# The hand-over from the Mamba stage to the expert stage: the plan of the early tiles, their loads and tile 0's first work are put into the last scan and into the last sequence's tail

## The chip, the cores and the metric

One core of a Trainium2 chip. The metric is device time in microseconds (us). Engines: PE is TensorE, DVE VectorE, ACT ScalarE, POOL GpSimd, SP SyncE, which here only issues DMAs.

## The reference

Eight sequences of 512 tokens with 256 channels. Cut to its order:

```
x = layernorm(x + mamba(x))      # mamba ends in a layernorm of its own:
    # project in, 4-tap convolution, silu; B, C and dt from it
    # h[t] = h[t-1] * exp(dt*A) + dt*B*x;  y = sum over 16 states of h*C + x*D
    # y * silu(gate), project out, + x, layernorm
x = layernorm(x + ffn(x))        # 8 experts, top 4 of them for each token:
    # out = down(min(gate,7) * sigmoid(1.702*gate) * (clip(up,-7,7)+1)), weighted, summed
```

## The kernel before

It has three stages. **Stage 1** (to about 590 us) works by rounds, `ROUNDS`, from -1 to 9 (`r.like`), each of 16 slots `t`. In round r sequence r is scanned (`r.b`), r+1 is projected in (`r.a`), r-1 is projected out and normed twice (`r.c`), and r-2 is routed to its experts (`r.d`). Rounds 8 (`SEQS`) and 9 (`LAST`) scan nothing: they are the tail of the last two sequences. Each engine has a hand-written order over rounds and slots; semaphores tie the engines together. In a slot DVE weighs the inputs of one of the 16 states (`weigh_inputs`) and scans it (`scan`), POOL multiplies the state by C (`read_state`), and PE sums (`sum_states`). The weights of experts and the rows of tile 0 share memory with what stage 1 uses: `first_raw`, `first_wh` and `first_wl` hold the input and two of the four broadcast rings (`bc`).

Routing of a sequence: transposes of its normed rows (`transpose_rows`), router product (`route`), ranking on DVE (`rank_experts`), a count over tokens on PE (`count`, `take_counts`), places in the experts' queues (`places`), and sixteen indirect DMAs by POOL that scatter its rows to the queues in device memory (`scatter`). `while_scanning` makes POOL wait at some slots so that it doesn't run beside certain DVE work.

**Stage 2** takes the queues in tiles of 512 rows of one expert (36 tiles in these runs, in pairs; the first `EARLY` = 4 are written out, the rest is a loop). For each tile SP loads its expert's weights and rows (`load_weights`, `load_rows`). Products are made in split precision: ACT copies a value to fp32r (`copy_weights`, `copy_tile`, `copy_product`) and DVE subtracts for the remainder (`rest_of_...`), and PE multiplies high by high, high by low and low by high. A tile has four chunks of up-projection (`up_projection`, read by `read_gate`, `read_up`; `clip_up`, `product_of_chunk` on DVE) and four of down-projection. DVE reads the output (`read_output`), ACT weighs it, POOL adds it to `total` with four indirect adds (`add_output`). DVE's copy of a tile's token numbers, `copy_tokens`, waits for the adds of the tile two before.

Which expert and which rows tiles 0 to 3 take is worked out on DVE by `plan_early`, from the counts of the first `EARLY_SEQS` = 6 sequences, by some 16 small steps that each wait for the one before; `plan_rest` plans the others in stage 2. The early tiles hold only full tiles. The constants for it (`c_tile`) are loaded over a buffer of stage 1. At the end of each order:

```
for _ in range(12): next(plan)        # DVE, round 8, slot 0: 12 steps of plan_early
weave(plan)                           # DVE, round 8, slot 2, behind the gate
if r.d and t == (4 if r.last else 3): count(r)       # PE, ahead of project_out at slot 3
LAST_SCATTERS = {6: (0,), 7: (1,), 10: (2,), 12: (3,), 13: range(4, TT * TOPK)}   # POOL
```

`weave` runs several chains of steps in turn. **Stage 3** (from about 1302 us) is the last layernorm, sequence by sequence.

## Time and profile before

| | us |
|---|---|
| median of 3 runs | 1333.25 (1333.24 to 1339.11) |
| the profiled execution | 1337.31 |
| its span, first to last instruction | 1335.5 |
| busy: PE, DVE, ACT, POOL | 1170.2, 1048.7, 896.6, 745.3 |

Busy times are sums over the span. The end of the last scan is at 572.4 us of the span, the first down-projection at 631.0 and the first add to `total` at 661.6. Times in the text without another unit are us from the start of that span.

### The profile page before, as it was taken

The page shows a single profiled execution, that of the slowest core. Times are in us where ns is not written, and L with a number is a line of the kernel's source. Part 1 is how long each engine was busy: PE and PEld are TensorE (multiplying, and loading weights), DVE is VectorE, ACT ScalarE, POOL GpSimd, SP SyncE. Part 2 cuts the span into 40 slices and gives each one's busy share as a digit, 9 for nine tenths or more (in the row PEclk, how much of TensorE's full clock was granted, in tenths as well). Part 3 has the DMA queues.
Part 4 walks back from the last instruction along what each step waited for, and adds up shares of the span by engine and source line. Part 5 has one row for each costly group of instructions (what it writes and reads, how often), then busy time and mean ns, then how long its engine had stood idle before and what let it go on. Part 6 is the DMA issues. An engine that isn't in the chain of part 4 may idle for free. (4 is left out here: it accounts for less than half of the span.)

```text
span 1335.5 us, 17897 instructions
## 1 busy us (share of the span) xinstructions
PE 1170.2 (88%) x5138; PEld 805.3 (60%) x5138; DVE 1048.7 (79%) x1791; ACT 896.6 (67%) x1551; POOL 745.3 (56%) x566
## 2 busy tenths in 40 slices
PE   7879897979898897676899999999999999999940
PEld 3324353534353434245788888888888888888830
DVE  2999999999999999964777667777677777766734
ACT  3785959495959585516577766777676777766734
POOL 0356567888787878967633444443444433444442
PEclk9899998999999898977899999999999999999975
DMA  2543444445454545354866556556556566556637
GB/s 74 217 179 127 154 148 177 176 166 187 173 191 172 192 154 181 127 192 157 315 164 161 133 139 165 160 162 162 128 140 167 160 162 163 138 135 161 162 36 252
DMA packets 69260, 217.21 MB, mean 163 GB/s; under 512 B 7520, under 2 KB 43232, under 8 KB 56288
## 3 DMA queue, kind: packets, MB, share of 16 engines
q1 hardware_dynamic: 29664, 167.42, 34.4%
q0 software_dynamic: 26880, 36.72, 16.1%
q10 hardware_dynamic: 12672, 12.58, 2.9%
q8 instruction: 16, 0.26, 0.1%
q14 instruction: 28, 0.23, 0.0%
HBM read 165.54 MB, written 51.15 MB: 162 GB/s over the span
## 5 line engine op out<-in xcount | busy, mean ns | idle before, releaser
L640 PE MATMUL p_y<-read,small 128*128 128x512 f32 x512 | 257.8, 642 | 58.2 <-POOL read L1187 58.2
L1051 DVE TENSOR_TENSOR_SCAN state<-decay,p_bu 128x512 f32<-128x512 f32 x256 | 297.3, 1203 | 1.5 <-issue 1.5
L1511 POOL DMA_INDIRECT total<-o_v,tok x144 | 267.4, 1857 | 44.1 <-issue 44.0
L640 PEld LDWEIGHTS p_y<-read,small 128*128 128x128 f32 x512 | 101.3, 205 | 199.5 <-issue 116.8
L1509 POOL TENSOR_TENSOR scrap<-neg_half 128x1 f32<-128x1 f32 x36 | 13.6, 379 | 319.9 <-ACT o_v L1418 317.3
L824 ACT ACTIVATE decay<-dt,scan_rate 128x511 f32<-128x511 f32 x256 | 164.3, 710 | 10.1 <-DVE state L1051 9.8
L504 ACT ACTIVATE gate_v<-p_g,bias 128x512 f32<-128x512 f32 x144 | 98.4, 683 | 102.8 <-PE p_up L494 97.7
L1229 POOL DMA_INDIRECT queues<-rows,index x128 | 133.4, 1042 | 32.5 <-issue 29.2
L1405 ACT ACTIVATE ah<-a_v 128x512 fp32r<-128x512 f32 x144 | 91.1, 633 | 89.6 <-DVE a_v L518 85.9
L1187 POOL TENSOR_TENSOR read<-state,bc 128x1024 f32<-128x1024 f32 x64 | 127.5, 2004 | 20.7 <-DVE p_bu L1042 8.4
L512 DVE TENSOR_SCALAR up_v<-up_v 128x512 f32<-128x512 f32 x144 | 61.4, 427 | 68.5 <-ACT up_v L507 65.9
L1456 DVE TENSOR_TENSOR al<-a_v,ah 128x512 fp32r<-128x512 f32 x144 | 98.8, 686 | 12.4 <-ACT ah L1405 12.4
L518 DVE SCALAR_TENSOR_TENSOR a_v<-gate_v,up_v 128x512 f32<-128x512 f32 x144 | 99.7, 693 | 4.9
L507 ACT ACTIVATE up_v<-p_up,bias 128x512 f32<-128x512 f32 x144 | 98.2, 682 | 0.0
L1187 POOL TENSOR_TENSOR read<-state,first_wh 128x1024 f32<-128x1024 f32 x32 | 64.0, 2001 | 59.6 <-DVE p_bu L1042 53.8
L1187 POOL TENSOR_TENSOR read<-state,first_wl 128x1024 f32<-128x1024 f32 x32 | 63.9, 1997 | 39.9 <-DVE p_bu L1042 15.6
L1378 PE MATMUL p_o<-first_wh,ah 128*128 128x256 f32 x288 | 82.6, 287 | 2.3 <-DVE al L1456 2.3
L1378 PE MATMUL p_o<-wh,ah 128*128 128x256 f32 x288 | 81.9, 284 | 1.7 <-DVE al L1456 1.7
L1042 DVE TENSOR_TENSOR p_bu<-p_u,bc 128x512 f32<-128x512 f32 x128 | 81.3, 681 | 0.0
L1378 PE MATMUL p_o<-first_wl,ah 128*128 128x256 f32 x288 | 80.8, 281 | 0.0
L1378 PE MATMUL p_o<-first_wh,al 128*128 128x256 f32 x288 | 80.8, 281 | 0.0
L1378 PE MATMUL p_o<-wh,al 128*128 128x256 f32 x288 | 80.3, 279 | 0.0
(220 smaller groups left out, 3017.6 us busy)
## 6 DMA issues: line engine op xcount, KB each, us to landing
bc<-bc_rows SPq DMA_DIRECT2D x32, 1024.0 KB, 4.7
first_raw<-in_w_experts SPq DMA_DIRECT2D x19, 1668.0 KB
raw_w<-in_w_experts SPq DMA_DIRECT2D x18, 1668.0 KB
first_wh<-bc_rows SPq DMA_DIRECT2D x16, 1024.0 KB
first_wl<-bc_rows SPq DMA_DIRECT2D x16, 1024.0 KB
first_rows<-queues SPq DMA_DIRECT2D x19, 544.0 KB
xq<-queues SPq DMA_DIRECT2D x18, 544.0 KB
queues<-pad SPq DMA_DIRECT2D x9, 544.0 KB
```

Source lines behind the costliest of these rows:

```text
L504: act.activation(gate_v[i % 2][:, :], p_g[i % 2][:, :], ACT.Silu, bias=bias[t.p][:, 0, i:i + 1], scale=ALPHA)
L507: act.activation(up_v[i % 2][:, :], p_up[i % 2][:, :], ACT.Identity, bias=bias[t.p][:, 1, i:i + 1])\
L518: dve.scalar_tensor_tensor(a_v[i % 2][:, :], gate_v[i % 2][:, :], TOP, up_v[i % 2][:, :], ALU.min, ALU.mult)\
L640: mm = pe.matmul(p_y[h][:, :], ident[:, :], read[:, t % 4, h, :], start=False, stop=(t == SLOTS - 1))
L824: act.activation(decay[t % AHEAD][:, h, 1:LEN], dt[s.p][:, h, 1:LEN], ACT.Exp, scale=rate[:, h, t:t + 1])\
L1051: dve.tensor_tensor_scan(state[t % 4][:, h, :], decay[t % AHEAD][:, h, :], p_bu[:, h * LEN:(h + 1) * LEN], 0.0, ALU.mult, ALU.add).then_in ...
L1187: pool.tensor_tensor(read[:, t % 4, :, :], state[t % 4][:, :, :], of_state(t, 1), ALU.mult).then_inc(s_read, 1)
L1229: pool.indirect_dma_start(queues, bass.IndirectOffsetOnAxis(ap=index[s.p][:, i:i + 1], axis=0), rows[s.p][:, i // TOPK, :], None).then_inc ...
L1378: mm = pe.matmul(to, v[:, i, a * P:(a + 1) * P], w[t.p][:, c:c + D], start=(i == 0 and a % 2 == 0 and m == 0), stop=(i == CH - 1 and m == ...
L1405: act.activation(ah[:, i, :], a_v[i % 2][:, :], ACT.Copy).then_inc(s_ah, 1)
L1456: dve.tensor_tensor(al[:, i, :], a_v[i % 2][:, :], ah[:, i, :].bitcast(F32), ALU.subtract).then_inc(s_al, 1)
L1511: pool.indirect_dma_start(total, bass.IndirectOffsetOnAxis(ap=tok[t.p][:, a:a + 1], axis=0), o_v[t.p][:, a, :], None, compute_op=ALU.add). ...
```

## The change

- **Plan**: five sequences, not six, fill the early tiles. `plan_early` is woven with `rank_experts` in round 7 (the last scan), slot 2; POOL waits there for its end (`s_tables`). `c_tile` is loaded in that scan, ahead of its fifth broadcast.
- **Tile 0's loads** are issued when SP has done the last scan's broadcasts; writing the spare rows goes behind the loads of tiles 0 and 1.
- **Tile 0's work**: ACT copies its weights at the start of round 8, DVE's remainders, the tile's transposes and its split follow in slots 0 to 3; all four chunks of up-projection (`AHEAD_OF_LOOP = CH`) are issued on PE in slot 4 of round 8, behind `count`, which is behind `project_out` now. The first two are read at slot 6, the others in round 9, where three products are split too. Two of three parts of tile 1's weights are also done before stage 2.
- **POOL**: two scatters of sequence 5 go from the last slot of round 7 to behind the reads in round 8.

The helpers `copy_product` and `rest_of_product` are moved out of stage 2's functions unchanged.

```diff
         d, a, c = self.d, self.a, self.c
-        return (["tr0", "tr1", "rt"] * d + ["in0", "in1"] * a + ["cnt"] * d + ["o0", "o1"] * c + ["cv0", "cv1"] * a
-                + ["dt0", "dt1", "bc", "in2", "in3"] * a)
+        scanning, over = d and self.b, d and not self.b
+        return (["tr0", "tr1", "rt"] * d + ["in0", "in1"] * a + ["cnt"] * scanning + ["o0", "o1"] * c + ["cnt"] * over
+                + ["cv0", "cv1", "dt0", "dt1", "bc", "in2", "in3"] * a)
...
-EARLY, EARLY_SEQS = 4, 6
+EARLY, EARLY_SEQS = 4, 5
 assert EARLY_SEQS * LEN * TOPK - E * (TILE - 1) > (EARLY - 1) * TILE
...
-        dve.wait_ge(s_tload, 16)
+        dve.wait_ge(s_dt, SEQS)
         dve.memset(one_row[:, :], 1.0)
...
         yield from steps.step(dve.tensor_tensor(early_first[:, :], early_upto[:, :], full_e[:, :], ALU.subtract))
+        dve.wait_ge(s_tload, 16)
         yield from list_tiles(dve, steps, 0, EARLY, early_upto, early_first, early_first)
...
-    AHEAD_OF_LOOP = 2
+    AHEAD_OF_LOOP = CH
...
                     sum_states(r.s.at(-1), SLOTS - 2 + t)
-                if r.last and t == 0:
-                    transpose_tile(pe, Seq(0, 0))
-                    up_projection(pe, Seq(0, 0), 0)
                 if r.d and t == 0:
...
                     route(r)
+                if r.like == SEQS and t == 2:
+                    pe.wait_ge(s_bu, halves_done(r.s, -1))
+                    transpose_tile(pe, Seq(0, 0))
                 if r.a and t == 2:
...
                     project(r, 1)
-                if r.last and t == 4:
-                    up_projection(pe, Seq(0, 0), 1)
-                if r.d and t == (4 if r.last else 3):
+                if r.d and r.b and t == 3:
                     count(r)
...
                     project_out(r, 1)
+                if r.d and not r.b and t == 4:
+                    count(r)
+                if r.like == SEQS and t == 4:
+                    for i in range(AHEAD_OF_LOOP):
+                        up_projection(pe, Seq(0, 0), i)
                 if r.a and t == 4:
...
+                if r.like == SEQS and t == 3:
+                    act.wait_ge(s_y, SEQS)
+                    for k in range(KD):
+                        copy_tile(act, first, k)
+                if r.last and t == 3:
+                    copy_product(act, first, 0)
+                    copy_product(act, first, 1)
+                    for i in (2, 3):
+                        read_gate(act, first, i)
+                        read_up(act, first, i)
+                    copy_product(act, first, 2)
                 if r.d and t == 3:
...
-                if r.like == SEQS and t == 8:
-                    act.wait_ge(s_y, SEQS)
+                if r.like == SEQS and t == 0:
+                    act.wait_ge(s_read, SLOTS * (SEQS - 1) + 4 * RING - 4)
                     for i in range(3):
-                        copy_weights(act, Seq(0, 0), i)
-                    for k in range(KD):
-                        copy_tile(act, Seq(0, 0), k)
+                        copy_weights(act, first, i)
+                if r.last and t == 0:
+                    copy_weights(act, second, 1)
                 if r.d and t == 0:
...
                     store_x1t(r, 1)
-                if r.last and t in (1, 4):
-                    read_gate(act, Seq(0, 0), t // 4)
-                    read_up(act, Seq(0, 0), t // 4)
                 if r.a and t == 2:
...
                     apply_norm(r.s.at(-1), 0, z, s_normed1)
+                if r.like == SEQS and t == 6:
+                    for i in (0, 1):
+                        read_gate(act, first, i)
+                        read_up(act, first, i)
+                    copy_weights(act, second, 0)
                 if r.like == Round.FIRST and t == 7:
...
         plan = plan_early(dve, plan_steps)
+        early, second = Seq(0, 0), Seq(0, 1)
         for r in ROUNDS:
             for t in range(SLOTS):
-                if r.like == SEQS and t == 0:
-                    for _ in range(12):
-                        next(plan)
                 if r.like == Round.FIRST and t == 2:
...
                     gate(r)
-                if r.like == SEQS and t == 2:
-                    weave(plan)
-                if r.last and t == 1:
-                    clip_up(dve, Seq(0, 0), 0)
-                    product_of_chunk(dve, Seq(0, 0), 0)
                 if r.d and t == 2:
                     route_steps = Steps(dve, s_route, r.s.at(-2).n, ROUTE_STEPS)
-                    weave(rank_experts(r, route_steps))
-                if r.d and t == (5 if r.last else 3):
+                    weave(rank_experts(r, route_steps), *[plan] * (r.like == SEQS - 1))
+                if r.like == SEQS and t == 0:
+                    for i in range(2):
+                        rest_of_weights(dve, early, i)
+                if r.like == SEQS and t == 2:
+                    rest_of_weights(dve, early, 2)
+                if r.like == SEQS and t == 3:
+                    for k in range(KD):
+                        rest_of_tile(dve, early, k)
+                    read_bias(dve, early)
+                if r.like == SEQS and t == 10:
+                    for i in (0, 1):
+                        clip_up(dve, early, i)
+                        product_of_chunk(dve, early, i)
+                    rest_of_weights(dve, second, 0)
+                if r.last and t == 3:
+                    rest_of_weights(dve, second, 1)
+                    rest_of_product(dve, early, 0)
+                    rest_of_product(dve, early, 1)
+                    for i in (2, 3):
+                        clip_up(dve, early, i)
+                        product_of_chunk(dve, early, i)
+                    rest_of_product(dve, early, 2)
+                if r.d and t == (3 if r.b else 5):
                     take_counts(r, route_steps)
...
                     make_padding(dve)
-                if r.last and t == 0:
-                    for i in range(2):
-                        rest_of_weights(dve, Seq(0, 0), i)
-                    for k in range(KD):
-                        rest_of_tile(dve, Seq(0, 0), k)
-                    read_bias(dve, Seq(0, 0))
                 if r.last and t == 5:
...
                 pool.wait_ge(s_rexp, 2 * r.s.at(-2).n + 1)
+            if r.like == SEQS - 1 and t == 2:
+                pool.wait_ge(s_tables, 1)
             if r.d and t == 6:
...
             for t in range(SLOTS):
-                if r.d and r.b and t in SCATTERS:
+                if r.d and r.b and t in SCATTERS and not (r.like == SEQS - 1 and t == SLOTS - 1):
                     scatter(r.s.at(-2), SCATTERS[t])
...
                 if r.like == SEQS and t == 0:
-                    scatter(r.s.at(-3), range(9, TT * TOPK))
+                    scatter(r.s.at(-3), range(SCATTERS[SLOTS - 1][0], TT * TOPK))
                 if r.c and t == 6:
...
             for pair in range(PAIRS):
+                if i == SEQS - 1 and pair == RING:
+                    sp.wait_ge(s_u, SEQS)
+                    sp.dma_start(c_tile.rearrange("p a b -> p (a b)"), ins["tile"]).then_inc(s_tload, 16)
                 if r.b:
...
             for i in range(CH):
-                if i > 0:
-                    copy_product(t, i - 1)
-                elif later:
-                    copy_product(t.at(-1), CH - 1)
+                if later:
+                    copy_product(act, t.at(-1) if i == 0 else t, (i - 1) % CH)
                 if later or i >= AHEAD_OF_LOOP:
...
                     copy_share(t, expert)
-                if i == 0:
+                if i == 0 and later:
                     copy_weights(act, t.at(1), 0)
...
                         copy_tile(act, t.at(1), k)
-                    copy_weights(act, t.at(1), 1)
+                    if later:
+                        copy_weights(act, t.at(1), 1)
                 if i == 2 and later:
...
         end = Seq(ends[0], 1)
-        copy_product(end, CH - 1)
+        copy_product(act, end, CH - 1)
         weigh_output(end)
...
         plan = plan_rest(dve, plan_steps)
-
-        def rest_of_product(t, i):
-            n = CH * t.n + i
-            dve.wait_ge(s_ah, n + 1)
-            dve.tensor_tensor(al[:, i, :], a_v[i % 2][:, :], ah[:, i, :].bitcast(F32), ALU.subtract).then_inc(s_al, 1)
...
             for i in range(CH):
-                if later or i > 0:
+                if later:
                     clip_up(dve, t, i)
...
                     copy_tokens(t)
-                    rest_of_weights(dve, t, 2)
+                    if later:
+                        rest_of_weights(dve, t, 2)
                 if i == 1 and later:
...
                         rest_of_tile(dve, t.at(1), k)
-                if i == 2:
+                if i == 2 and later:
                     rest_of_weights(dve, t.at(1), 0)
...
                     read_bias(dve, t.at(1))
-                rest_of_product(t, i)
+                if later or i == CH - 1:
+                    rest_of_product(dve, t, i)
         assert next(plan, "end") == "end"
...
             for i in range(2):
-                sp.wait_ge(s_scat[i], 16 * TT * TOPK * (seqs // 2))
-
-        sp.wait_ge(s_u, SEQS)
-        sp.dma_start(c_tile.rearrange("p a b -> p (a b)"), ins["tile"]).then_inc(s_tload, 16)
+                sp.wait_ge(s_scat[i], 16 * TT * TOPK * ((seqs + 1 - i) // 2))
+
         sp.wait_ge(s_silu, 2 * SEQS)
...
         load_weights(sp, Seq(0, 0))
-        sp.wait_ge(s_ends, 2)
-        write_spare_rows(sp)
         scattered(EARLY_SEQS)
...
         load(Seq(0, 1))
+        sp.wait_ge(s_ends, 2)
+        write_spare_rows(sp)
         for t in tiles(sp, ends):
```

## Rows read from the trace of the kernel before

**Rows 1.** Waits, 710 to 1290: engine, line <- releaser: us, times, longest.

```profile
POOL scrap L1509 <- ACT o_v L1418: 291.6, 32, 9.2
...
DVE tok L1461 <- DMA total<-o_v,tok: 93.2, 31, 3.7
```

**Rows 2.** Timeline of DVE: start, us, work [idle before <- releaser].

```profile
707.70 0.17 DVE L1461 CAST tok<-first_rows 128x4 uint32<-128x4 int32 x1 [2.78 <-DMA total<-o_v,tok]
```

**Rows 3.** Instructions of line L1461: ns min/median/max, first to last start.

```profile
L1461 DVE CAST tok<-xq x18: 165/170/172, 649.3 to 1271.6; 128x4 uint32<-128x4 int32 x18
```

**Rows 4.** Timeline of POOL, last sequence's scatters and first add.

```profile
628.97 0.99 POOL L1229 DMA_INDIRECT queues<-rows,index  x1 [0.16 <-issue]
...
651.72 0.96 POOL L1229 DMA_INDIRECT queues<-rows,index  x1 [0.30 <-issue]
...
660.33 1.08 POOL L1509 TENSOR_TENSOR scrap<-neg_half 128x1 f32<-128x1 f32 x1 [7.65 <-ACT o_v L1418]
```

**Rows 5.** Timeline of DVE around the last scan's end.

```profile
570.11 2.31 DVE L1051 TENSOR_TENSOR_SCAN state<-decay,p_bu 128x512 f32<-128x512 f32 x2
...
572.96 6.64 DVE L426 CAST rest<-used_i 128x8 f32<-128x8 int32 x1
...
581.75 1.29 DVE L1059 TENSOR_TENSOR y<-p_y,sg 128x512 f32<-128x512 f32 x2
...
583.54 0.23 DVE L416 CAST row_i<-rest 128x4 int32<-128x4 f32 x1
```

**Rows 6.** Timeline of POOL around the last scan's end.

```profile
567.22 3.96 POOL L1187 TENSOR_TENSOR read<-state,bc 128x1024 f32<-128x1024 f32 x2
...
573.65 3.96 POOL L1187 TENSOR_TENSOR read<-state,bc 128x1024 f32<-128x1024 f32 x2
```

**Rows 7.** Timeline of PE between the stages.

```profile
569.28 8.41 PE L640 MATMUL p_y<-read,small 128*128 128x512 f32 x12 [2.29 <-POOL read L1187]
...
577.53 1.04 PE L664 MATMUL p_bank<-small,rows 128*128 128x128 f32 x8
...
580.12 1.85 PE L674 MATMUL p_bank<-small,x1t 128*128 128x8 f32 x16
...
586.11 2.05 PE L597 MATMUL p_bank<-w,y 128*128 128x256 f32 x4
...
594.05 1.03 PE L597 MATMUL p_bank<-w,y 128*128 128x256 f32 x4
...
595.22 0.70 PE L656 MATMUL p_bank<-x,small 128*128 128x256 f32 x2
...
640.54 0.76 PE L494 MATMUL p_g<-xh,wh 128*128 128x512 f32 x1 [4.21 <-issue]
```

**Rows 8.** Groups of DVE instructions, 672 to 1300: xcount | busy, mean ns.

```profile
L1456 DVE TENSOR_TENSOR al<-a_v,ah 128x512 fp32r<-128x512 f32 x136 | 93.3, 686 | 12.0 <-ACT ah L1405 12.0
...
L468 DVE TENSOR_TENSOR wl<-raw_w,wh 128x1024 fp32r<-128x1024 f32 x51 | 60.9, 1222 | 0.2
```

**Rows 9.** Windows: us, busy by engine, then PEclk, DMA share, GB/s.

```profile
590.00:592.00 2.00, 2.00 (x6) 1.04 (x5) 0.00 (x0) 0.00 (x0) 0.00 (x0) 0.50 0.99 379
```

**Rows 10.** Timeline of ACT and POOL at the last sequence's second norm.

```profile
606.87 1.11 POOL L1197 TENSOR_TENSOR neg_16th<-row_sum,norm_c 128x4 f32<-128x4 f32 x1 [0.26 <-DVE z L1067]
...
613.00 2.08 ACT L861 ACTIVATE rows<-z,neg_mean,rstd 128x256 f32<-128x256 f32 x4 [1.78 <-POOL neg_mean L1206]
```

**Rows 11.** Timeline of DVE around the last ranking.

```profile
620.11 0.57 DVE L512 TENSOR_SCALAR up_v<-up_v 128x512 f32<-128x512 f32 x1 [9.51 <-ACT up_v L507]
...
621.32 0.18 DVE L1075 TENSOR_TENSOR lg<-p_bank,small 128x32 f32<-128x32 f32 x1
...
627.91 0.18 DVE L1160 CAST index<-spot_sum 128x16 uint32<-128x16 f32 x1
```

**Rows 12.** Timeline of SP's queue in the last scan.

```profile
507.56 7.54 SPq L1321 DMA_DIRECT2D bc<-bc_rows  x2
```

**Rows 13.** DMA issues, 480 to 680: KB each, us to landing.

```profile
expo<-in_tile SPq DMA_DIRECT2D x1, 168.0 KB, 5.1
```

More of the change, by code:

```diff
@@ L519, in product_of_chunk, with copy_product @@
            .then_inc(s_a, 1)
+    def copy_product(act, t, i):
+        n = CH * t.n + i
+        act.wait_ge(s_a, n + 1)
+        after(act, s_down, n - CH + 1)
+        act.activation(ah[:, i, :], a_v[i % 2][:, :], ACT.Copy).then_inc(s_ah, 1)
     def copy_tile(act, t, k):
@@ L530, in rest_of_tile, with rest_of_product @@
            .then_inc(s_xl, 1)
+    def rest_of_product(dve, t, i):
+        n = CH * t.n + i
+        dve.wait_ge(s_ah, n + 1)
+        dve.tensor_tensor(al[:, i, :], a_v[i % 2][:, :], ah[:, i, :].bitcast(F32), ALU.subtract).then_inc(s_al, 1)
     def read_bias(dve, t):
@@ L734, in act_stage1 @@
     def act_stage1(act):
+        first, second = Seq(0, 0), Seq(0, 1)
         def load_table(func):
@@ L1399, in act_stage2 @@
         ends = []
-        def copy_product(t, i):
-            n = CH * t.n + i
-            act.wait_ge(s_a, n + 1)
-            after(act, s_down, n - CH + 1)
-            act.activation(ah[:, i, :], a_v[i % 2][:, :], ACT.Copy).then_inc(s_ah, 1)
         def copy_share(t, expert):
@@ L1451, in dve_stage2 @@
         plan = plan_rest(dve, plan_steps)
-        def rest_of_product(t, i):
-            n = CH * t.n + i
-            dve.wait_ge(s_ah, n + 1)
-            dve.tensor_tensor(al[:, i, :], a_v[i % 2][:, :], ah[:, i, :].bitcast(F32), ALU.subtract).then_inc(s_al, 1)
         def copy_tokens(t):
```

## Prediction

> **What bounds the kernel now.** I read the waits of the second stage first. Over nearly all of it POOL waits for the scaled output of a tile, and DVE waits for earlier adds to land before it copies the next tile's token numbers [rows 1]. The timeline of one tile shows that this is a closed loop: DVE's copy at 707.7 is released by the landing of an add [rows 2]; behind it in DVE's order stands the reading of the tile before, which ACT scales and POOL adds, and the landing of that releases the next such copy. The copies of tiles 1 and 35 are 622.3 us apart, 18.3 us a tile [rows 3]. No other engine closes that period: so the second stage ends at the time of its first add plus a fixed number of periods, and the change, which touches none of the loop's members, is worth what it does to the **first add**. The reader is to look at what releases that add: before, POOL has sat idle for 7.65 us, waiting for tile 0's output, when it starts at 660.33; its sixteen scatters of the last sequence ran from 628.97 to 652.7 [rows 4]. So two chains arrive there: the scatters, and tile 0.
>
> **The change, part by part.**
>
> *The plan moves into the scan.* Before, it starts as the last scan ends (572.4) and its last step is at 583.5 with the gate's two products in between; of that span 6.64 is one cast [rows 5]. That cast lies under POOL's two last reads and the operation behind them [rows 6]. Without the stall (6.5) and the gate (1.2) the plan is 11.2 + 0.2 - 6.5 - 1.2 = 3.7, plus the hand-overs around it. In the scan DVE is never idle, so all of it moves the scan's end, less a few tenths for being woven into the ranking. I take **3.8 later** (bounds: 3.0 if the weaving hides the ranking's share, 4.8 with a scatter's length, about 1 us, of stall). POOL is held until the plan is done, so no read can lock the casts out; it resumes with DVE, as it did, and I charge nothing more.
>
> *Behind the scan.* The reads of the last two states stood behind two scatters, from 571.2, when the reads before end, to 573.65 [rows 6]. These scatters now follow the reads. But PE is the later one: its sums of three states run from 569.28 to 577.7 at a slow clock, so the last sum, which ends as the router product starts at 580.1, comes only some 0.1 sooner than the shift [rows 7]: 583.8. DVE's subtraction of the early weights (two halves, 1.22 each [rows 8]) meets these reads. The long cast shows what happens: DVE waited until 579.6, through all that POOL had lined up [rows 5, 6]. Here DVE would wait to 580.9 and be done at 583.3, before the last sum. I charge nothing; if that cover fails, up to 2.4. The Trainium skill (SBUF — State Buffer, Who interferes with whom) says that a DVE instruction with two SBUF inputs and a GpSimd one that reads SBUF exclude each other for one whole instruction, whoever starts first. By that rule DVE could get in between two reads and put the last read off by 1.2 to 2.4, which speaks against the change; the last sum would then still start within 0.3 of the same time, since PE has the sum before it and the transposes to do.
>
> The gate ends at 585.1, 2.1 later than before. Then the gain: before, PE stood idle from 582.0 to 586.1, for the ranking and the count, and projected from 586.1 to 595.9, more than half of it at a clock of 0.5 [rows 7, 9]. Now the count stands behind the projection, and the router product (1.85) and tile 0's transposes (1.1, eight of them, like the eight of 577.53) fill PE until 586.7. PE has then been busy without a gap since the sums, so I take the full clock that it had reached by 580: the last quarter of before, 594.05 to 595.9, is 1.7 and a tail of 0.15, four are 6.9, and end at **593.6, 2.3 earlier**. At the slow clock it is 9.8, ending at 596.5, 0.6 later.
>
> *Norms of the last sequence.* From there to the end of the second norm took 19.2 (595.9 to 615.1 [rows 7, 10]). Added: the index of sequence 6 now waits for the late count, and POOL's first scatter of it stands ahead of the reciprocal root, 0.6. Removed: the mean's two small products took 1.1 each, as the first shows [rows 10], under DVE's subtraction of the weights; now a shorter clip is there, -1.2. So 612.2, 2.9 earlier. The first two chunks lie in this stretch in which PE was idle. The other two wait for ACT to read the first pair after the first norm; they restart after an idle of 4 us, one of them slow, and end at about 612, just as the transposes of the last sequence are due.
>
> *The last ranking.* Before, 6.2 passed from the norm to the ranking's first operation at 621.32, since ACT and DVE had the first chunk in front of it [rows 10, 11]. The clip and product just ahead of it (1.2, from 620.11) are gone from there, and I take 0.6 off for the end of the first chunk on PE, which the transposes had to wait for: 4.4, 616.6. From there to the index took 6.8 [rows 11]. Now DVE has, between ranking and counts, one half of the weights (1.2), three product remainders (0.6 each with overlap [rows 8]) and two clips with products (1.1 each, 620.11 to 621.32 with a slower start [rows 11]), 5.2 where it waited 2.6 for the count: 9.4. The index comes at **626.0, 2.1 earlier**. POOL's scatters of sequence 6 have to be gone by then; they start behind the second power, 2.9 earlier, and before they ended exactly when the last sequence's began. Before, 24.1 passed from POOL's small operation ahead of the first of them (628.6) to the last one's end [rows 4]; 626.0 + 0.2 + 24.1 gives POOL free at **650.3**.
>
> *Tile 0 and 1.* Tile 0 now has three of four products split before the stage begins, and the early weights of tiles 0 and 1 are done; only tile 1's x remainder stands between the index and tile 1's first chunk: 626.0 + eight plan steps at 0.23 (3.7 over 16 steps) 1.8 + the token copy 0.1 + two remainders 1.3 = 629.2, against 640.54 [rows 7]. Tile 0's output follows from it at the old distance, 19.8 to POOL's start at 660.33 [rows 4]: 649.0. That is before 650.3, by 1.3. All loads of SP (weights 0, rows 0, weights 1) are asked sooner than before and are behind nothing new except the small table.
>
> **The sum.** The first add goes from 660.33 to 650.3: 7.65 of idle gone and the scatters 2.4 earlier, together 10.0. The profiled execution took 1337.31 with a span of 1335.5; the median shown is 1333.25, 4 below it and within its runs' spread. The gain is taken off the median: **1323.2**.
>
> **Rivals.**
> 1. *Tile 0 binds*, or the scatters go faster: the last sequence's sixteen took 1.48 each, 23.7 from the first start to the last end [rows 4]; if the new ones are 10% quicker, POOL is free at 647.9 and tile 0's 649.0, or 647 if PE's chunks run fast, sets the start: gain 11.3 to 13.3, 1320 to 1322. For: one scatter alone is 0.96 long, so they do wait for something. Against: these writes move with them. Chance 0.13.
> 2. *PE's clock stays at 0.5 in the projection*, or 2 to 3 us are lost in one of the new orders (DVE's 5.2 ahead of the counts is the nearest): the index comes at 628 to 629 and the gain is POOL's idle alone, 7: 1326. For: the clock was 0.5 behind an idle of 4 us [rows 7, 9]. The Trainium skill (TensorE: Matmul & The Clock Gate, HAM oscillation — how this bites in real kernels) says the same, that PE, after a gap, works its next burst slowed; by it the four chunks in two bursts pay twice. Against: no such gap is left ahead of the projection. Chance 0.20.
> 3. *The DMAs.* Eight padding writes, weights and rows of tiles 2 and 3 now fall on more of the scatters. At 1.7 to 1.85 a scatter instead of 1.48, POOL is free at 654 to 656: gain 4 to 6, 1328. Chance 0.12.
> 4. *No effect*: the loop isn't closed by the adds in the first tiles, and tile 1's chain, 1.3 ahead of the scatters here, is really held at its old place. Against: the wait of each following tile names the adds. Gain under 3: 1332. Chance 0.07.
> 5. *Slower.* The table of tile numbers lands late. It is asked behind the fourth broadcast, whose issue ends at 515.1, and takes 5.1 to land [rows 12, 13]: 520.3, and the plan wants it about 1.5 later. DVE waits there with the scan behind it, so each us goes straight to the end. It takes all of the gain only if it lands after 532, and shows as slower than 0.5% after 538: 1334 to 1345. Chance 0.06.
>
> **How the numbers follow.** My forecast (gain 8.5 to 11.4) has 0.42; its own range is 1321.5 to 1325. About 0.5% (6.7 us) is what a measurement of this kernel can tell from no change. Faster by more: my case, rival 1, and most of rival 2 (0.13), 0.68. Within: the rest of rival 2, rivals 3 and 4, 0.26. Slower: 0.06. The range 1319 to 1330 leaves out rivals 4 and 5 and the tails of 1 and 3, about 0.18.
>
> **What would show it.** In the new profile: no cast over 1 in the plan and the scan's last operation 3.8 later; the projection ended near 593.6 at a clock of 1.0; the last index near 626; POOL's idle ahead of its first add gone, or nearly so, with the last scatter just in front; that add near 650.3, and 18.2 a tile after it. The prediction is wrong if DVE idles in the last scan (rival 5), if POOL still waits for tile 0, or if the first token copy that waits isn't released by an add.

## Result, and the profile after

The changed kernel takes 1329.01 us, the median of 20 executions (1324.2 to 1337.13), against 1335.94 (1332.93 to 1341.28) for 20 of the kernel before, taken beside it: a ratio of 0.995, with a 95% interval of 0.9935 to 0.9964. That is 6.9 us faster where the forecast said 10.0. The time lies in the range of 1319 to 1330, which was set against a median of 1333.25; the kernel before read 2.7 more in the larger set. Taken as gains from 1333.25 that range is 3.3 to 14.3, so 6.9 lies in it as well. The gain of 10.0 doesn't lie in the measured interval, 4.8 to 8.7.

The profiled execution of the changed kernel took 1335.48, span 1333.6, and is one of the slowest of its 20. It is the profile of the change, so it comes first; one of an execution of the same kernel that took 1323.89 comes in the experiments. The steps at the end of the scan went as forecast. Timeline of DVE:

```profile
576.62 6.89 DVE L470 TENSOR_TENSOR first_wl<-first_raw,first_wh 128x1024 fp32r<-128x1024 f32 x2
584.36 1.29 DVE L1089 TENSOR_TENSOR y<-p_y,sg 128x512 f32<-128x512 f32 x2 [0.85 <-PE p_y L653]
...
619.08 0.19 DVE L1105 TENSOR_TENSOR lg<-p_bank,small 128x32 f32<-128x32 f32 x1 [10.00 <-PE p_bank L687]
...
628.37 0.17 DVE L1199 CAST index<-spot_sum 128x16 uint32<-128x16 f32 x1
```

No plan step stands there any more. In its place the two halves of the early weights take 6.89 where they need 2.35: the stall has moved from the plan's cast [rows 5] to this subtraction, as the prediction said, and it is hidden, since DVE, done at 583.5 (forecast 583.3), then waits 0.85 for PE all the same. POOL's order beside it:

```profile
571.48 7.85 POOL L1226 TENSOR_TENSOR read<-state,bc 128x1024 f32<-128x1024 f32 x4
579.30 1.99 POOL L1259 TENSOR_TENSOR x<-x,small 128x1024 f32<-128x1024 f32 x1
...
628.97 0.99 POOL L1268 DMA_INDIRECT queues<-rows,index  x1 [0.15 <-issue]
...
648.15 0.96 POOL L1268 DMA_INDIRECT queues<-rows,index  x1 [0.30 <-issue]
658.91 0.61 POOL L1543 TENSOR_TENSOR scrap<-neg_half 128x1 f32<-128x1 f32 x1 [9.81 <-ACT o_v L1456]
```

The last scatters take 20.1 (628.97 to 649.11), less than the 23.7 of [rows 4]. But POOL then idles 9.81 for tile 0's output, although tile 0 was meant to be early: the first add is at 658.91 and not at the 650.3 of the forecast. PE shows why:

```profile
586.77 1.03 PE L610 MATMUL p_bank<-w,y 128*128 128x256 f32 x4
...
593.05 0.70 PE L669 MATMUL p_bank<-x,small 128*128 128x256 f32 x2
...
642.49 0.28 PE L1422 MATMUL p_o<-first_wh,ah 128*128 128x256 f32 x1 [1.14 <-issue]
...
649.47 0.37 PE L1422 MATMUL p_o<-first_wl,ah 128*128 128x256 f32 x1 [1.03 <-issue]
```

The projection is right: four parts in 7.0, from 586.77 to 593.75, at a granted clock of 1.00 where [rows 9] had 0.50. The windows view of the stretch:

```profile
590.00:592.00 2.00, 2.00 (x10) 1.42 (x9) 0.68 (x4) 0.84 (x4) 1.42 (x2) 1.00 0.95 371
```

But from 640.06 to 651.60 PE gets through seven more recorded matmuls of tile 0's third down-projection, 1.0 to 2.1 us apart, and is idle in between for nothing that the profile can name ("issue"). In the same stretch SP spends 21.06 on issuing the eight padding writes:

```profile
630.95 21.06 SPq L577 DMA_DIRECT2D queues<-pad  x8
```

Whether this belongs to the change or to the execution is the first thing that the experiments ask. The second is why the gain is 6.9 and not 10.

### The profile page after: what moved, and what is told of

It reads as the page before. It is cut to its first block and busy times, and to the rows that moved or that the text cites. A ratio compares the mean times of both kernels' runs of the same rounds, so it can differ in the third digit from the quotient of the medians.

```text
span 1333.6 us, 17900 instructions
## 1 busy us (share of the span) xinstructions
PE 1165.7 (87%) x5138; PEld 803.6 (60%) x5138; DVE 1046.4 (78%) x1791; ACT 896.5 (67%) x1551; POOL 739.9 (55%) x566
## 5 line engine op out<-in xcount | busy, mean ns | idle before, releaser
L653 PEld LDWEIGHTS p_y<-read,small 128*128 128x128 f32 x512 | 100.6, 203 | 205.6 <-issue 112.2
L841 ACT ACTIVATE decay<-dt,scan_rate 128x511 f32<-128x511 f32 x256 | 164.3, 710 | 17.1 <-DVE state L1081 16.9
L527 ACT ACTIVATE ah<-a_v 128x512 fp32r<-128x512 f32 x144 | 91.0, 633 | 90.1 <-DVE a_v L520 83.6
L1226 POOL TENSOR_TENSOR read<-state,bc 128x1024 f32<-128x1024 f32 x64 | 127.3, 2000 | 22.4 <-DVE p_bu L1072 10.9
L514 DVE TENSOR_SCALAR up_v<-up_v 128x512 f32<-128x512 f32 x144 | 61.4, 426 | 65.4 <-ACT up_v L509 64.5
L1422 PE MATMUL p_o<-first_wh,ah 128*128 128x256 f32 x288 | 83.5, 290 | 6.3 <-DVE al L543 3.5
L1226 POOL TENSOR_TENSOR read<-state,first_wl 128x1024 f32<-128x1024 f32 x32 | 63.9, 1996 | 40.0 <-DVE p_bu L1072 17.1
```

The lines of the kernel that those rows point to most:

```text
L527: act.activation(ah[:, i, :], a_v[i % 2][:, :], ACT.Copy).then_inc(s_ah, 1)
L653: mm = pe.matmul(p_y[h][:, :], ident[:, :], read[:, t % 4, h, :], start=False, stop=(t == SLOTS - 1))
L841: act.activation(decay[t % AHEAD][:, h, 1:LEN], dt[s.p][:, h, 1:LEN], ACT.Exp, scale=rate[:, h, t:t + 1])\
L1226: pool.tensor_tensor(read[:, t % 4, :, :], state[t % 4][:, :, :], of_state(t, 1), ALU.mult).then_inc(s_read, 1)
L1422: mm = pe.matmul(to, v[:, i, a * P:(a + 1) * P], w[t.p][:, c:c + D], start=(i == 0 and a % 2 == 0 and m == 0), stop=(i == CH - 1 and m == ...
```

## Experiments

Times are read behind the end S of the last scan, since the first stage alone moves by up to 4 us from one execution to the next. The length of that scan, from its drive product (`p_u`) to S, stands in the second column. "Gate" is the end of the gate's products on DVE, "projected" the end of the projection out on PE, "last index" the end of the last sequence's index. All of the table is read from the timelines of DVE, POOL and PE of each profiled execution; "add 0" is the first add, "copy 2" and "copy 3" are the token copies of the third and fourth tile, which wait for landed adds.

| kernel | scan | gate | projected | last index | scatters end | add 0 | copy 2 | copy 3 |
|---|---|---|---|---|---|---|---|---|
| before | 65.8 | 10.6 | 23.5 | 55.7 | 80.3 | 87.9 | 99.4 | 117.4 |
| b_same | 65.9 | 10.6 | 22.4 | 52.0 | 84.1 | 84.1 | 94.6 | 112.7 |
| b_plan | 68.7 | 7.9 | 19.0 | 49.3 | 83.0 | 83.0 | 93.0 | 111.1 |
| b_count | 65.4 | 10.6 | 19.3 | 49.6 | 83.3 | 83.3 | 93.4 | 111.4 |
| b_plan_count | 68.7 | 7.9 | 15.1 | 45.9 | 71.7 | 75.6 | 86.7 | 104.7 |
| b_ends_late | 65.8 | 10.6 | 22.4 | 52.0 | 85.4 | 85.5 | 99.4 | 117.3 |
| after | 68.7 | 9.0 | 17.1 | 51.8 | 72.4 | 82.2 | 93.4 | 111.4 |
| a_same | 68.7 | 8.0 | 16.0 | 48.2 | 74.9 | 74.9 | 85.3 | 103.3 |
| a_count_old | 68.8 | 9.0 | 18.6 | 51.0 | 74.2 | 74.2 | 84.2 | 105.8 |
| a_ends_late | 68.7 | 8.1 | 15.8 | 48.7 | 72.9 | 73.0 | 86.8 | 104.8 |
| a_ends_twice | 68.8 | 8.0 | 15.9 | 48.8 | 73.2 | 83.5 | 93.7 | 116.0 |
| a_adds_early | 68.8 | 8.0 | 16.0 | 48.1 | 85.1 | 68.0 | 79.1 | 99.0 |
| a_both | 68.8 | 8.1 | 16.1 | 43.5 | 84.5 | 67.3 | 78.5 | 101.7 |
| a_weights_ahead | 68.7 | 8.0 | 16.0 | 48.1 | 83.6 | 67.2 | 78.9 | 100.6 |

**Is the starved PE part of the change?** The changed kernel was run again as it is, and with the padding writes moved or doubled, and the kernel before with them moved. Ratios are to the kernel before run beside each.

The kernel as it is, a_same:

> The changed kernel again, for the spread of one thing: in its first profile PE issued 16 instructions of tile 0's third down-projection chunk in 11.5 us (640.1 to 651.6, one about every 0.7 or 1.4), with nothing in the profile that it waited for, while SP issued the eight padding writes. Theory A (traffic): that gap is there in every execution, its length changes from run to run, and it is what spreads the times over 13 us. Theory B (an accident of one execution): it is mostly gone here. Under both the median is 5 to 8 us under the kernel before, and without the gap the first add stands at 648 to 650.

The eight padding writes one tile later, a_ends_late (and in the kernel before, b_ends_late); the two writes of spare rows get a semaphore of their own, so that the first add doesn't wait for the padding:

```diff
-            if isinstance(t.half, int) and t.n == 1:
+            if isinstance(t.half, int) and t.n == 2:
                 sp.wait_ge(s_ends, 3)
                 write_ends(sp, range(E))
```

> The changed kernel with its eight padding writes of the queues' ends issued behind the loads of tile 3 instead of those of tile 2, and the first add no longer waiting for them. Theory A (the padding writes starve PE of instructions): the gap of 11 us behind tile 1's first chunks goes, the first add stands at 648 to 650, and the time is 3 to 8 us under a_same, unless the same gap comes back beside the moved writes, then behind 655, where the adds' loop hides about 3 us of it. Rival (the gap belongs to that place in PE's program, or to the sixteen scatters): the gap stays at 640 and the time is a_same's within 1.5.

> The kernel before with the same late padding writes. Theory A: before had little of that gap (PE idle 4.2 at 640, which tile 1's weights explain), so 0 to 3 us faster than before at most. Then the change itself, measured between the two kernels with late padding, is worth about 10 us, as the forecast had it, and the missing 3 us are the gap. Rival: the two differ by 5 to 7 us as the unmodified pair does, and the missing gain is elsewhere.

The padding twice, a_ends_twice; the second eight go to a tensor that nobody reads:

```diff
                 write_ends(sp, range(E))
+                for e in range(E):
+                    sp.dma_start(sink[e * TILE:(e + 1) * TILE, :].rearrange("(p a) c -> p a c", a=SUBS), pad[:, :, :])\
+                      .then_inc(s_pad, 16)
```

> The changed kernel with eight more writes of 544 KB from the same padding tile to an unused part of device memory, right behind the eight. Theory A: the gap on PE grows by as much as the writes take longer, 8 to 12 us, and the first add, which waits for them too, comes at 668 or later: 6 to 12 us over a_same. Rival (the writes have nothing to do with it): the gap keeps its length; the first add is held only by the wait for the 16 writes, if they land after 659.

Measured: a_same 1323.72 against 1330.84 of the kernel before on the same chip, ratio 0.9942 (0.9923 to 0.9962), 7.1 faster. a_ends_late 1325.99 (0.9954, 0.9939 to 0.9969), a_ends_twice 1336.03 (1.0035, 1.0018 to 1.0053), b_ends_late 1337.59 (1.0044, 1.0027 to 1.006).

In the profiled execution of a_same PE isn't starved and SP needs 11.50 for the eight writes. Timeline of POOL, a_same:

```profile
621.54 0.99 POOL L1268 DMA_INDIRECT queues<-rows,index  x1
626.15 0.99 POOL L1268 DMA_INDIRECT queues<-rows,index  x1 [3.62 <-issue]
...
646.83 0.96 POOL L1268 DMA_INDIRECT queues<-rows,index  x1 [0.30 <-issue]
647.82 0.24 POOL L1543 TENSOR_TENSOR scrap<-neg_half 128x1 f32<-128x1 f32 x1
```

The first add follows the last scatter with no idle time. DVE starts to read tile 0's output at 63.0 behind S; from there to POOL's add 4.8 pass in b_plan_count, so tile 0 has some 7 us of slack, and the scatters set the first add. The starvation is in one of the eight profiles of the changed kernel and its variants. It is no fixed part of the change, and its cause stays open. The first theory for a_same, that it is in every execution, is out.

Nor is the padding a cost that moving it would save. Moved back, it falls on the adds: from the first add to the copy that waits for its landing 10.4 passed in a_same and 13.8 in a_ends_late. By the medians 2.3 is lost here, which the intervals don't tell from nothing, and 6.8 in the kernel before, which they do; b_ends_late was expected to be up to 3 faster. Between the two kernels with late padding the medians differ by 11.6, close to the 10 that the first theory expected there, but since the kernel before got slower and not since a loss went away. Doubled, the padding costs 12.3. Waits of a_ends_twice, 640 to 700 us:

```profile
DVE tok L1494 <- DMA total<-o_v,tok: 21.6, 2, 18.5
...
PE p_x L481 <- DMA xq<-queues: 17.0, 1, 17.0
```

PE waits 17.0 for the rows of a tile, queued behind the writes, where a_same waits 3.6. So the first theory, padding as the thing that ate the missing 3 us, isn't borne out: moving these writes back won nothing in either kernel. No run leaves them out, so what they cost where they are is not shown.

**Is the kernel before as its profile shows it?** b_same is the kernel before again, beside three variants of the changed kernel.

> The kernel before again, for a second profile of it, since the times of one kernel spread over 9 us. My sum took the first add from one execution, 87.9 us behind the end of its last scan (572.4), and b_ends_late, which is the same up to there, had it 85.5 behind. Theory (the sum started from a slow execution): the first add stands 84.5 to 86.5 behind the scan's end here, POOL's idle ahead of it is under 5, and the gain of the change, 143.6 from the last drive to the first add in a_same, is 7 to 8, not 10. Rival (the profiled execution was typical): 87 to 89, idle 7 or more.

Measured 1331.16 against 1330.64 (1.0001, 0.9986 to 1.0015). Its profiled execution was 7.3 quicker than the first profile of the same code, and differs from it in the very rows of [rows 4]. Timeline of POOL, b_same:

```profile
623.99 1.39 POOL L1229 DMA_INDIRECT queues<-rows,index  x1 [0.16 <-issue]
632.33 1.12 POOL L1229 DMA_INDIRECT queues<-rows,index  x1 [6.95 <-issue]
...
651.41 1.43 POOL L1229 DMA_INDIRECT queues<-rows,index  x1 [0.30 <-issue]
652.87 0.25 POOL L1509 TENSOR_TENSOR scrap<-neg_half 128x1 f32<-128x1 f32 x1
```

There is no idle time of POOL ahead of the first add, where [rows 4] have 7.65. Instead there is one of 6.95 between the first and the second scatter of the last sequence. The index is at 52.0 and not 55.7. POOL is 3.3 behind it with the last sequence's first scatter, since it is still at sequence 6's. The same picture, a pause of 6.75 to 6.95 and no wait for tile 0, is in the profiles of b_ends_late, b_plan and b_count. So four of the six profiles of the kernel before and its variants show it, and the one on which the prediction was built doesn't. The padding isn't the cause: in b_ends_late it is issued from 644.07 on, and the pause is there.

What goes with the pause is SP's load of the third tile's weights (1668 KB). Timeline of SP, b_same:

```profile
622.91 0.34 SPq L543 DMA_DIRECT2D first_raw<-in_w_experts  x1
624.05 0.34 SPq L552 DMA_DIRECT2D first_rows<-queues  x1
```

and of a_same, where that load is asked 28 us sooner, since the early weights are split sooner:

```profile
595.04 0.34 SPq L556 DMA_DIRECT2D first_raw<-in_w_experts  x1
622.26 0.34 SPq L565 DMA_DIRECT2D first_rows<-queues  x1
```

Where these weights are asked about 1.1 us ahead of the first scatter (b_same, b_ends_late, b_plan, b_count), the second scatter comes 8.1 to 8.3 after the first; where they are asked with it or behind it (the first profile before, b_plan_count), 2.6 to 2.9; where they were loaded long before (all kernels built on the changed one), 1.4 to 4.9. No kernel moved this load alone, so that it causes the pause is argued and not shown; nor is it shown why the pause varies from 0.44 to 3.9 among the kernels built on the changed one.

**Which part of the change does it?** First, the changed kernel with the count of sequence 6 back ahead of the projection out, a_count_old:

```diff
-                if r.d and r.b and t == 3:
+                if r.d and not r.last and t == 3:
                     count(r)
...
-                if r.d and not r.b and t == 4:
+                if r.last and t == 4:
                     count(r)
```

> The changed kernel with the count of sequence 6 back ahead of the projection (on PE, on DVE and in the order of the PSUM banks). The forecast gave this move 2.3 us together with the full clock. Theory: PE waits about 1.3 for the ranking ahead of the count and keeps its clock, so the projection ends about 1.5 later and the index 0.5 to 1 later: 0 to 1.5 us slower than a_same. Rival (without the move PE's clock falls as before and the projection ends 5 later): 3 to 4 us slower.

It took 1327.0 (0.9968, 0.9951 to 0.9984). That is 3.4 more than a_adds_early and 3.5 more than a_both, which ran beside it and stand for a_same (1323.72, another chip) as shown below; the intervals overlap, so a cost of the old place is likely and not certain. The projection ends at 18.6 behind S, where it ends at 16.0 in a_same and at 17.1 in the change's first profile, whose gate is as late as here: 1.5 to 2.6 are PE's wait for the ranking. Its four parts take 7.0 here too, so the clock is not what the count's place decides. The profiled execution took 1330.99, the slowest of its 12, and in it the later index doesn't reach the first add: the scatters behind it take 22.7 and not 26.3, and the add comes at 74.2, 0.7 sooner than in a_same. The delay is behind that add, where copy 3 comes 2.5 later than in a_same and PE waits longer for the rows of a tile than the 3.59 of a_same. Timeline of PE, a_count_old:

```profile
656.73 1.97 PE L480 MATMUL p_x<-small,xq 128*128 128x128 f32 x8 [5.28 <-DMA xq<-queues]
```

So this profile doesn't show that the count's place costs anything by way of the last index.

Then, from the other side, the kernel before with the plan's part alone (b_plan), with the count's place alone (b_count), and with both but nothing of tile 0's work moved (b_plan_count). In short:

```diff
-EARLY, EARLY_SEQS = 4, 6
+EARLY, EARLY_SEQS = 4, 5
...
-                    weave(rank_experts(r, route_steps))
+                    weave(rank_experts(r, route_steps), *[plan] * (r.like == SEQS - 1))
```

```diff
-                if r.d and t == (4 if r.last else 3):
+                if r.d and t == 3 and r.like < SEQS:
                     count(r)
                 if r.c and t == 3:
                     project_out(r, 0)
                     project_out(r, 1)
+                if r.d and t == 4 and r.like >= SEQS:
+                    count(r)
```

> The kernel before with the plan's part of the change alone: five sequences for the early tiles, the plan woven with the ranking in the last scan, its table loaded in that scan, POOL's wait, and two scatters moved behind the reads. The count, tile 0's work and SP's other orders stay as before. Theory: what counts is when the last index is ready. The last scan gets 2.9 us longer; the plan's 10 us behind the scan are gone, but only 2.6 of them lay on the path (gate at 8.0 behind the scan's end and not 10.6), because the projection stands behind the ranking and the count. So all comes 2.6 sooner behind a scan end that is 2.9 later: no change, 1331 within 1.5, and the index 49.4 behind the scan's end. Rival (the plan alone makes most of the gain, since the ranking too starts sooner and takes the projection with it): 1325 to 1327.

> The kernel before with one thing changed: in round 8 the count and the places of sequence 6 go behind the projection out. Theory: PE projects right behind the gate, at 18.6 behind the scan's end and not 22.4, and the last index, and with it the last scatters and the first add, come about 3 us sooner: 1328. Rival (the count only pays where PE has tile 0's transposes to keep busy with before it; here PE idles ahead of the gate, the clock is at half, and 8 us of projection eat the gain): 1330.5.

> Both parts together, and nothing of tile 0's work moved: tile 0's transposes, its split, its four chunks and tile 1's weights stand where they stood before. Theory (the last index and the sixteen scatters behind it set the first add; tile 0 has slack either way): index about 46 behind the scan's end, since the work that the change puts in front of the last counts is missing, first add 71 to 75 behind it, time 1321 to 1324.5, as fast as the whole change. Rival (tile 0 and tile 1 have to come sooner too): their chain binds, and the time is 1328 to 1331.

Measured, against 1330.62: b_plan 1332.76 (1.0007, 0.9989 to 1.0024); b_count 1327.78 (0.9992, 0.9976 to 1.0007); b_plan_count 1327.8 (0.9987, 0.9972 to 1.0002). None of the three can be told from no change by its ratio, though the medians of the last two are 2.8 lower. For the plan that was the expectation: all that follows comes 2.7 sooner behind a scan that is 2.8 longer. The count alone was expected to bring 3; its index comes 2.4 sooner, but POOL is still at sequence 6's scatters, the last sixteen take 30.2 where b_same has 28.9, and the first add comes 0.8 sooner. b_plan_count came out near the rival's 1328 and not at the theory's 1321 to 1324.5. Its scatters end at 71.7 as promised, but then tile 0 binds. Timeline of POOL, b_plan_count:

```profile
642.49 1.48 POOL L1228 DMA_INDIRECT queues<-rows,index  x1 [0.30 <-issue]
647.88 0.61 POOL L1513 TENSOR_TENSOR scrap<-neg_half 128x1 f32<-128x1 f32 x1 [3.91 <-ACT o_v L1422]
```

This is its fastest execution (1324.85), 1.0 above the profiled one of a_same; its median is 3 higher, and no profile shows what holds that. So in this execution tile 0's early work is what is missing, up to 3.9 at the first add. That it is only needed once the scatters end sooner fits b_same, where POOL doesn't wait for tile 0; the kernel before with tile 0's work alone was not run. None of the parts tried alone gives anything that its ratio tells from nothing, while the whole change does (a_same, 0.9942).

**Does the first add set the end?** POOL does ten of the last sixteen scatters, then tile 0's adds, then the other six, and the first add no longer waits for the padding (a_adds_early). In a_both DVE also takes the last counts ahead of the lot of products and weights that the change put in front of them.

```diff
             if r.last:
-                scatter(r.s.at(-2), range(TT * TOPK))
+                scatter(r.s.at(-2), range(FIRST_SCATTERS))
```

> The changed kernel with POOL's order changed in one place: ten of the last sequence's sixteen scatters, then tile 0's adds, then the other six; the first add waits for the spare rows alone and not for the padding of the queues. Theory (POOL's scatters set the first add, and the first add sets the end): tile 0's output is ready 66.5 behind the scan's end, so the first add comes there and not at 74.9, less 2 to 4 us that the adds take longer to land beside the padding: 4 to 8 us faster than a_same, about 1317 beside its 1323.7. Rival (something else holds the loop, the loads of tile 4 behind the last scatters above all): within 1.5 of a_same.

> As a_adds_early, and DVE works out the last sequence's counts, weights and index ahead of tile 0's product remainders and of chunks 2 and 3. Theory: the index comes 5 us sooner, but POOL is still at sequence 6's scatters then (they end 48 behind the scan), so the last scatters start at most 0.5 sooner; the early plan's successor, padding and token copy move 5 forward, tile 1's first chunk 2 to 4: the first add at 63 to 66 behind the scan, 0 to 3 us faster than a_adds_early. Rival (chunks 2 and 3 late cost as much as is won): 0 to 2 slower than it.

Measured: 1323.61 (0.9937, 0.9914 to 0.9961) and 1323.5 (0.9937, 0.9915 to 0.9959), both as a_same. The theory expected 1317, the rival the same as a_same. In a_adds_early the first add comes 7.0 sooner, copy 2 comes 6.2 sooner, but copy 3 only 4.3. Timeline of POOL, a_adds_early:

```profile
640.16 0.60 POOL L1546 TENSOR_TENSOR scrap<-neg_half 128x1 f32<-128x1 f32 x1 [3.38 <-ACT o_v L1459]
...
659.91 0.55 POOL L1546 TENSOR_TENSOR scrap<-neg_half 128x1 f32<-128x1 f32 x1 [2.67 <-ACT o_v L1459]
...
683.10 0.55 POOL L1546 TENSOR_TENSOR scrap<-neg_half 128x1 f32<-128x1 f32 x1 [14.49 <-ACT o_v L1459]
```

Three adds 19.8 and 23.2 apart; the third is at 683.10, as in a_same (110.9 behind S, 110.2 there). In a_both the index comes 4.6 sooner still, but the last sequence's first scatter is no sooner, at 48.8 behind S for 48.5. SP's waits in a_adds_early name what may have taken the gain back (590 to 690 us; in a_both the same wait is 19.2):

```profile
SPq L1588 <- DMA queues<-rows,index: 20.7, 1, 20.7
```

SP doesn't ask for anything of the fifth tile before the last scatter has landed, and the six scatters were put off. The last run asks for the fifth tile's weights ahead of that wait, a_weights_ahead:

```diff
                 sp.wait_ge(s_tables, 2)
+                load_weights(sp, t.at(1))
                 scattered(SEQS)
```

> The kernel with tile 0's adds ahead of the last six scatters, and the weights of tile 4 asked ahead of SP's wait for those scatters (its rows behind it). In the run before it the wait ended at 659.6, weights and rows were asked then, and PE waited 4.1 for the rows; the third tile's add came 23.2 behind the second's. Theory (these loads take back what the earlier adds give): the weights come some 8 us sooner, the rows land about 3 sooner, and 2 to 3 us of the 7 are kept: 1321 against 1323.6. Rival (the loop's buffers or the adds of tile 1, put off by six scatters, hold it): 1323.5, no change.

It took 1320.96 (5 executions, 1319.06 to 1324.05; 0.9944, 0.993 to 0.9957). The median is the lowest of all, but the ratio is that of a_same: no version here is shown to beat the changed kernel. The gap that was 23.2 is gone, and another has come ahead of it. Timeline of POOL, a_weights_ahead:

```profile
639.40 0.61 POOL L1546 TENSOR_TENSOR scrap<-neg_half 128x1 f32<-128x1 f32 x1 [2.65 <-ACT o_v L1459]
...
661.71 0.55 POOL L1546 TENSOR_TENSOR scrap<-neg_half 128x1 f32<-128x1 f32 x1 [5.86 <-ACT o_v L1459]
...
679.49 0.46 POOL L1546 TENSOR_TENSOR scrap<-neg_half 128x1 f32<-128x1 f32 x1 [9.07 <-ACT o_v L1459]
```

The third add is 3.6 sooner than in a_same here, 2.9 if counted from S. From there the tiles keep their pace. So the loads of the fifth tile were what made the 23.2, and part of the earlier first add is kept in this profile; whether it is in the median the ratio doesn't tell.

## Why the prediction was right, and where its size was off

**The frame held.** The second stage ends at its first add plus fixed periods. The waits of a_same, 710 to 1270 us, are those of [rows 1]:

```profile
POOL scrap L1543 <- ACT o_v L1456: 282.9, 31, 9.2
DVE tok L1493 <- DMA total<-o_v,tok: 93.7, 31, 3.7
```

From the fifth tile's token copy to the end of the span 626.2 to 629.5 pass in all fourteen profiles, while that copy itself stands between 691.0 and 709.6. The limit of the frame showed in a_adds_early: the loop carries an earlier first add only as far as the loads of the next tiles come too.

**The changed kernel was forecast well, by the profile of a_same.** From the start of the last scan the first add was to come after 143.7 (69.6 of scan and 74.1 behind it); a_same has 68.7 and 74.9, 143.6. Step by step, forecast and a_same: the plan lengthens the scan by 3.8, and by 2.8 to 2.9; the gate at 8.9 behind S, and 8.0; the projection ended at 17.4, and 16.0, at full clock; the last ranking at 40.4, and 38.7; the index at 49.8, and 48.2; the scatters done at 74.1, and 74.9, tile 0 ahead of them. The scatters took 26.3 where 23.7 were taken. In the change's own profile the prediction's sign of being wrong stood: POOL still waited for tile 0, 9.81, for the starved PE that no step of the prediction had. And the hit of 143.6 for 143.7 is partly luck: the scan came 0.9 shorter than forecast, the index 1.6 sooner behind it, and the scatters took 2.4 more.

**The term that was mis-sized is the starting point**: "7.65 of idle gone". POOL's idle time ahead of the first add stands in one of two profiles of the kernel before. In b_same the index came 3.7 sooner than in that profile and the first add 3.8 sooner, with the scatters up to it. Against b_same the sum is: scan +2.8, index 3.8 sooner, and from the index to the first add 26.7 for 32.1, 5.4 less; together 6.4, where 7.1 was measured and 10.0 forecast (+3.8, -5.9, -7.9). Most of the 3.6 between 10.0 and this sum of 6.4 is the 3.8 by which the first add stands later in the first profile than in b_same. The prediction took the term off the median, although it had noted that the profiled execution was 4 above it. That was against three executions; against the 20 of the larger set (1335.94) it is 1.4 above, and b_same is 1.1 under the median of its own set. So that the idle time is unusual is shown against the later sets (1330.6), where POOL waits for tile 0 in only one of the five profiles of the kernel before and its variants (b_plan_count's, 3.91); for the first set, which has no second profile of the kernel before and where 6.9 was measured all the same, it is argued.

So, between a_same and b_same, the gain has another make-up than told. It isn't idle time that goes. Of the 5.4 between index and first add, 2.8 are POOL's start, which stood behind sequence 6's scatters in b_same (3.3) and doesn't in a_same (0.4), and 2.6 are the sixteen scatters, 26.3 for 28.9; that comes from the shorter pause behind the first of them (3.6 for 6.95), whose cause is open. What each part of the change pays is shown less well: the count's place takes 1.5 to 2.6 off the projection, but a_count_old doesn't show it at the first add; the plan's place gains 2.7 and costs 2.8; without tile 0's early work POOL waits 3.9 in the fastest execution of b_plan_count.

**The rivals.** The first, tile 0 binding, is not so in a_same, and is so in the profile of the change, where PE is starved. The second, a slow clock in the projection, didn't happen in any profile of the changed kernel or its variants, not even in a_count_old. The third, slower scatters, happened in part: 1.64 each in a_same, with the pause, against 1.48 forecast, but 1.26 each in the changed kernel's first profile. For the fourth, no effect, nothing speaks: the ratio is clear of 1, and the token copies wait for landed adds. The fifth was out: DVE went through the plan without a pause. The lock between DVE and POOL was hidden, as its step said. The Trainium skill (SBUF — State Buffer, Who interferes with whom) lets either engine in after one whole instruction of the other. The trace doesn't agree with that: the record begins at 576.62, POOL's last operation ends at 581.29, and the two halves need 2.35 and end at 583.51, so DVE was held through the rest of the third read, the fourth and the operation behind them, more than one instruction. The prediction's own reading, DVE done at 583.3, was the right one.

## What to carry to other kernels

A profile is one execution: before a wait in it is booked as a gain, compare the profiled time with a median of more than three, and look at a second profile for the same wait, above all where two chains arrive within a few us of each other. Where two chains meet (here scatters and tile 0), moving one of them can leave the other to bind, as in b_plan_count, so the parts of such a change can't be priced one by one. An earlier start of a loop can be taken back by the loads of the following tiles, as the 7.0 of a_adds_early were by its third add.

## What the runs showed of the hardware

- PE fell to one recorded matmul per 1.0 to 2.1 us and SP to one DMA issue per 2.6 (1.3 to 1.5 in the other profiles), for 11 us or more, with nothing named that they wait for: in one profile of fourteen, at a DMA share of 0.32 to 1.02 over the stretch. The Trainium skill (Runtime: NRT & Kernel Launch, Instruction fetch mechanics) says that the engines' instructions come by DMA in blocks. The trace has such a packet where the slow stretch begins, in the DMA view of 640 to 641 us after:

```profile
q14 instruction: 1, 0.01, 1.9%
```

  Each of the fourteen profiles has 28 packets of this queue, five of them between 600 and 700 us, a_same at 633 and 642 among others, with no slow stretch behind them. So the packet explains nothing by itself, and this isn't settled.
- Sixteen scatters issued in a row by POOL take between 20.1 and 30.3 us. Most are 0.96 long and 0.30 apart; the rest is one pause behind the first (0.4 to 6.95) and single scatters of 1.4 to 2.0.
- From the first of four adds to the copy that waits for their landing 10.4 pass in a_same and 13.8 in a_ends_late, with the padding writes issued 25 us or 10 us ahead of the adds.
- The median of the kernel before is 1335.9 in the first set and 1330.6 to 1330.8 in the three later ones, on three chips. The 5 between them is nearly as much as the change is worth; only ratios taken side by side can tell it.
